# Sixteen-head cross-attentions: where the first scores of the second batch stand in the step that makes its queries

## What is computed

```
# first attention (L0): biases bq, bk, bv, bo and an additive mask; gate tanh(g_xattn[0])
qh = split_heads(layernorm(x) @ Wq.T + bq)      # (2, 16, 1024, 16)
kh = split_heads(ctx @ Wk.T + bk)               # (2, 16, 77, 16)
vh = split_heads(ctx @ Wv.T + bv)
attn = softmax(where(mask == 0, -inf, qh @ kh^T * 16**-0.5))
x = x + tanh(g_xattn[0]) * (merge_heads(attn @ vh) @ Wo.T + bo)
# last attention (L3): the same without biases and mask; gate tanh(g_xattn[3])
# behind each of the two stands a mixture-of-experts block on layernorm(x)
```

## Time and profile before

| what | us |
|---|---|
| median of 3 runs | 1196.19 (1195.82, 1196.19, 1201.35) |
| the profiled execution | 1195.52 |
| its span in the trace | 1193.4 |
| PE busy in the span | 1013.4 |
| DVE busy | 643.9 |
| ACT busy | 401.5 |

### The profile page before, as it was taken

How to read it: one execution, slowest core, us unless ns; L and a number is a source line. 1 busy time by engine, 2 the same in 40 slices (tenths; PEclk the granted TensorE clock), 3 DMA queues, 4 the chain that set the end, 5 groups by cost and what they waited for, 6 DMA issues and landing times. The chain is left out here.

```text
span 1193.4 us, 16543 instructions
## 1 busy us (share of the span) xinstructions
PE 1013.4 (85%) x5500; PEld 782.4 (66%) x5501; DVE 643.9 (54%) x1271; ACT 401.5 (34%) x638; POOL 255.4 (21%) x243
## 2 busy tenths in 40 slices
PE   5898999789999996766749559879898399999995
PEld 3677878578888873655637338748687266666663
DVE  5658759921232138777633478755675733333332
ACT  2544412111111127766520057544453021212220
POOL 3000001123544334300000000010000134444442
PEclk8899989989999999889965569997999599999998
DMA  4600131036666530000010200007112422222221
GB/s 130 194 1 19 36 107 36 23 117 170 198 189 176 149 89 0 1 1 1 1 37 1 70 1 1 2 5 289 37 37 72 159 35 47 45 44 44 44 44 23
DMA packets 67812, 79.63 MB, mean 67 GB/s; under 512 B 12656, under 2 KB 52171, under 8 KB 67755
## 3 DMA queue, kind: packets, MB, share of 16 engines
q1 hardware_dynamic: 54123, 60.27, 15.3%
q0 software_dynamic: 13632, 18.62, 9.1%
HBM read 60.73 MB, written 17.83 MB: 66 GB/s over the span
## 5 line engine op out<-in xcount | busy, mean ns | idle before, releaser
L2482 PE MATMUL ps<-w_L_ffn_w,f_xsT 128*128 x312 | 149.5, 603 | 0.7 <-DVE f_xsT L2644 0.6
L2278 DVE TENSOR_TENSOR f_h<-f_h,ps 128x1024 f32<-128x1024 f32 x24 | 29.3, 1220 | 111.1 <-PE ps L2074 57.9
L2446 POOL DMA_INDIRECT out_x<-f_yo,f_give x39 | 61.9, 1588 | 122.6 <-DVE f_yo L2661 119.7
L373 POOL TENSOR_TENSOR norm_vec<-norm_vec,npow 128x4 f32<-128x4 f32 (+2 forms) x25 | 25.3, 1013 | 288.8 <-DVE norm_vec L367 287.9
L2482 PEld LDWEIGHTS ps<-w_L_ffn_w,f_xsT 128*128 128x128 f32 x312 | 57.2, 194 | 42.6 <-issue 40.7
L2083 PE MATMUL ps<-b_room,f_h 128*128 128x256 f32 x384 | 85.0, 379 | 0.0
L2548 ACT ACTIVATE f_s<-ps 128x512 f32<-128x512 f32 x39 | 23.3, 597 | 181.9 <-PE ps L2482 181.9
L2083 PEld LDWEIGHTS ps<-b_room,f_h 128*128 128x128 f32 x384 | 72.9, 190 | 9.9
L534 PE MATMUL ps<-a_vblk,a_pT 128*128 128x51 f32 (+1 forms) x640 | 76.9, 277 | 0.0
L534 PEld LDWEIGHTS ps<-a_vblk,a_pT 128*128 128x128 f32 (+1 forms) x640 | 76.4, 197 | 0.0
L2497 PE MATMUL ps<-w_L_ffn_w,f_hT 128*128 x312 | 73.9, 380 | 0.9 <-DVE f_hT L2649 0.9
(11 more groups left out here) (376 smaller groups left out, 2098.9 us busy)
## 6 DMA issues: line engine op xcount, KB each, us to landing
w_L_ffn_w<-in_L_ffn_w SPq DMA_DIRECT2D x24, 512.0 KB, 8.2
b_room<-in_L_ffn_Wg SPq DMA_DIRECT2D x16, 512.0 KB, 4.6
b_room<-in_L_ffn_Wu SPq DMA_DIRECT2D x16, 512.0 KB, 6.0
b_room<-in_L_ffn_Wd SPq DMA_DIRECT2D x16, 512.0 KB, 6.0
xn_rows<-xn_sb SPq DMA_DIRECT2D x8, 512.0 KB, 2.9
x_sb<-in_x SPq DMA_DIRECT2D x4, 512.0 KB, 6.5
xn_sb<-in_L_ffn_w SPq DMA_DIRECT2D x2, 1024.0 KB, 7.6
x_sb<-acc_rows SPq DMA_DIRECT2D x4, 512.0 KB, 5.5
```

What stands on the lines that cost most here:

```text
L2278: dve.tensor_tensor(hT[p][:, :, :].rearrange("p a c -> p (a c)"), ge[p][:, :], ps[:, 2:4, :].rearrange("p a c -> p (a c)"), ALU.mult).then ...
L2446: pool.indirect_dma_start(out_rows[:, :], bass.IndirectOffsetOnAxis(ap=give[:, j:j + 1], axis=0), yo[j % 2][:, :], None, compute_op=ALU.ad ...
L2482: m = pe.matmul(ps[:, banks[p], :], xsT[p][:, i * P:(i + 1) * P], w[:, e, i, :], start=(i == 0), stop=(i == KT - 1))
```

## The change

On PE, `scores(8)` with its two waits moves in step 6 from behind `project(5)` to ahead of `values(6)`. On DVE, `front(8)` moves in step 6 from behind `residual(5)` to the head of the step, where `front` stands in all other steps; `add_bias(6)`, `normalise(6)` and `residual(5)` now follow it. Both `multihead` calls take the change. No instruction is added or removed, and ACT, POOL and SP issue what they did.

```diff
@@ PE, inside the loop over n
                     turn(n, (2,))
+                    if n == TB - 2:
+                        pe.wait_ge(s_kblk, KBLK + KT)
+                        pe.wait_ge(q_sb, 8)
+                        scores(n + 2)
                     values(n)
                     if ahead is not None:
                         ahead.tensor(pe, n, s_used)
                     if n:
                         project(n - 1)
-                    if n == TB - 2:
-                        pe.wait_ge(s_kblk, KBLK + KT)
-                        pe.wait_ge(q_sb, 8)
-                        scores(n + 2)
@@ DVE, inside the loop over n
-                    if n + 2 < NT and n != TB - 2:
+                    if n + 2 < NT:
                         front(n + 2)
                     if bo is not None:
                         add_bias(n)
                     normalise(n)
                     if n:
                         residual(n - 1)
-                    if n == TB - 2:
-                        front(n + 2)
                     if ahead is not None:
                         ahead.vector(dve, n)
```

## The result

| | before | after |
|---|---|---|
| median of 18 runs, us | 1196.08 | 1187.64 |
| lowest, highest | 1190.44, 1201.35 | 1182.51, 1194.08 |
| profiled execution | 1195.52 | 1189.43 |

What follows compares the result with a forecast made beforehand. PE was taken to bound the kernel, with 6.24 of its 14.6 us of waits for `front` in two gaps. Gains of 2.26 and 3.39 us, 5.65 in all, gave 1190.2 us, range 1187.8 to 1194.0.

Steps and rivals of the forecast that it cites:

- The gaps and what follows them: PE ahead of `scores(9)`, both attentions: gaps of 3.07 and 3.17 us go; `scores(9)` start at 91.43 and 858.02.
- The new wait at the router's transposes: L1309 of step 7: PE would newly wait about 0.8 us for DVE's series between `front(8)` and `front(9)`.
- The gain of the schedule: Both attentions, up to L1309 of step 7: 2.26 and 3.39 us gained, 1.23 of the latter being clock.
- The clock: Last attention, behind the gap: half clock took 5.82 us against 4.59 at full clock, so 1.23 us gained.
- Waits of under 1 us, so I take the full clock: Last attention: such waits replace the gap ahead of the clock's fall, so the stretch was priced at 4.59 us.
- The rival about the clock: Last attention: the fall may be missing in timed executions; gain there 2.16 us, sum 4.42, about 1191.5 us; chance 0.20.
- the case in which PE binds: Both attentions: DVE's series is shorter or overlaps, so PE sets both; gain 7.27 us, about 1188.6 us; chance 0.07.
- That it may be given back: Later stages wait for transfers or the clock restarts elsewhere, so most gain is lost: 1192 to 1195.5 us; chance 0.16.
- The slower rival: Later PE idles: clock rises fall elsewhere; five more half-clock stretches, 6.15 us against 5.65, some 1197 us; chance 0.07.

Runs made afterwards that it cites:

- e4_rows_late: Changed kernel with DVE's two passes of L386 of step 6 moved behind `front(9)`; ratio 0.9900 against the kernel before, median 1185.83 us.
- the filler: Kernel before, order unchanged, with twelve products that nothing reads on PE behind `scores(8)` of step 6; ratios 0.9971 and, run again, 0.9963.
- e12_rows_late_again: Same kernel as e4_rows_late, run again on one chip with three others; ratio 0.9915 against the kernel before.
- e7_dve_only: Kernel before with only the change's two DVE lines, `front(8)` at the head of step 6, PE as before; ratio 1.0004.

## Why the prediction was wrong

- *The gaps and what follows them:* right. By the sum `scores(9)` of the first attention start 91.43 - 86.92 = 4.51 us behind `scores(8)`, and 90.86 - 86.35 = 4.51 were measured; in the last one 858.02 - 854.02 = 4.00 and 4.04. (The query copies end 86.92 - 85.88 = 1.04 us ahead of `scores(8)`; "a second earlier" in the prediction is a slip for a microsecond.)
- *The new wait at the router's transposes,* 0.8 us forecast: right. The idle before them is 0.60 and 0.65 us, and e4_rows_late, in which the wait is gone, has them 0.77 and 0.81 us sooner. The series on DVE took 93.61 - 90.75 = 2.86 us against 2.95 in the first attention, 857.70 - 855.18 = 2.52 against 2.61 in the last. The late rows shorten the series and remove the wait; so it was DVE that held PE. That VectorE takes its instructions strictly in order (the Trainium skill, TensorE: Matmul & The Clock Gate, Architectural detail) agrees with it: the scores of `front(9)` were ready at 90.86 + 1.48 = 92.34, and L717 started only at 93.61, behind the passes of L386.
- *The gain of the schedule,* 2.26 + 3.39 less 1.23 for the clock, 4.42 us: 13.05 - 10.72 = 2.33 in the first place, and against the filler's last place, which has the old order and the full clock, 12.02 - 9.77 = 2.25. 4.58 us, right.
- *The clock* is the term that was mis-sized: 1.23 us in the sum, 2.6 us measured in the traces, and some 3.1 us by the estimate from all executions. The sum took the one profiled execution for all: no fall behind the first gap, one of 1.23 us behind the last. In seven traces with the old order the clock fell behind the first gap five times, at a mean cost over all seven of 14.39 - 13.05 = 1.34 us. Behind the last gap it fell seven times, at 13.59 - 12.02 = 1.57 us up to the end of the place and 19.90 - 18.02 = 1.88 to step 8. The kernel with the filler, which moves nothing, gained 3.5 and 4.4 us in time and 2.8 us by its places.
- *"Waits of under 1 us, so I take the full clock"* held in three of five traces behind the first place's new wait and in all five behind the last one's. The two falls are 1.6 us each, 17.85 - 17.21 = 0.64 us on average: 1.34 + 1.88 - 0.64 = 2.58 us for the clock, and with the schedule's 4.58 the 7.16 us of the table.
- *The rival about the clock* pointed the wrong way. It saw that the fall is a matter of chance in a single execution and concluded that it might be missing where it had been seen. The other half of the same thought, that it might come where it had not been seen, got one clause and no price: with falls of equal size behind both gaps the sum would have been 4.42 + 2 x 1.23 = 6.9 us, 1189.0, and a longer fall in one more. The lower end of the range, 1187.8, came from the case in which PE binds, whose 7.27 us hold the one fall of 1.23 and no other.
- *That it may be given back* later: only the two falls of 1.6 us behind the new wait were. From the router's transposes in the last place to the end it took 325 to 328 us in every trace.
- *The slower rival* asked for five more stretches at half clock. The changed kernel spent less time there, not more: 222.2 us against 232.1.

That the time fell below the range by 0.16 us only is partly luck of that comparison: its 9.2 us is the largest of the four, and the medians of the later three, 1189.52, 1189.00 and 1190.28, lie within the range. The clock's term was too small in any case.

What stays open: 8.0 us by all executions against 7.2 or 7.5 by the traces is within the scatter. The filler gained 0.7 to 1.6 us more than its places show and the late rows 1.1 to 2.9 us more; the rest of their span was 1164.5 to 1165.7 us in four traces against 1166.1 to 1171.3 in six of the kernel before. The time at 0.50 of all executions covers most of this, but it does not say where in the program it was saved. Whether an idle gap in the first attention also lengthens later stages, through where the clock's falls lie, was not settled.

The version with late rows (e4_rows_late, e12_rows_late_again) beats both kernels: medians 1185.83 and 1184.82 us in six runs each, and on the chip that ran both its mean lies 4.4 us below the changed kernel's, with 2.3 to either side, where the places give 1.58.

## What to carry to other kernels

Where a gap on TensorE is removed, price it as its length plus the clock falls behind it, and take how often these come from several traces: one execution shows one draw. Read on behind the place as well, for a short wait that the change brings can have a fall behind it. When a pass moves to the head of a step, add up what is now queued between it and the next pass of its kind, for that series sets the next wait; here moving 1 us of it away in each attention shortened the two places by another 1.6 us together. To learn what the clock alone costs, keep the engine busy in the gap with work that nothing reads.

## What the runs showed of the hardware that was not expected

An idle of 3.06 to 3.18 us on PE, the same to a hundredth in every trace, was followed by the 1.2 GHz level in twelve of fourteen cases, fourteen of sixteen with the two of e7_dve_only. A fall cost between 1.2 and 5.7 us up to step 8. In two of five traces the level came behind a wait of only 0.61 us, and in none of five behind one of 0.64 to 0.65 us in the last attention. The Trainium skill (TensorE: Matmul & The Clock Gate, What's actually happening) says that the monitor runs freely and doesn't start with the kernel; the different costs of one gap in different traces agree with that. Two traces of one binary on one chip had spans of 1188.1 and 1181.5 us, with their two places alike to 0.01 us: in a program with many falls of the clock a single execution tells a change of 5 us from nothing only in the place where it happens and right behind it.
